# Expert rows scaled at their tile and scatter-added into one sum over a copy of x, output projections moved to the next even unit

## The reference

```python
xn = (x - mean) / sqrt(var + 1e-5)
# local attention: 16 heads of 16, windows of 128 tokens at a stride of 64
qkv = xn @ w_qkv + b_qkv
for each window:  ow = softmax(q k^T / 4) v
attn = (concat(windows) @ w_out + b_out)[:, :512]
# 8 experts of width 512, the best 2 of each row
p, i = softmax(top_k(xn @ gate_w.T, 2))
h1, h2 = split(xn @ w12[e].T)
y = sum over the row's two experts e of p_e * ((silu(h1) * h2) @ w3[e].T)
out = x + attn + y
```

## Time and profile before

| | |
|---|---|
| median of 3 runs | 704.5 us (704.3 to 704.83) |
| the profiled execution's own time | 704.97 us |
| its span | 703.2 us |
| busy: PE, PEld, DVE, ACT, POOL | 630.0, 509.7, 567.5, 513.2, 281.5 us |
| instructions: PE, DVE, ACT, POOL | 5914, 902, 882, 330 |
| memory read, written | 58.93, 32.83 MB |

### The profile page before, as it was taken

The page is one execution under the profiler, slowest core; times in us unless marked ns, Lnnn a source line. Parts: engine busy times, 40 slices in busy tenths (PEclk is TensorE's granted clock), DMA queues, the critical chain, the costliest instruction groups (busy, mean ns, idle before and its releaser), DMA issues.

```text
span 703.2 us, 17940 instructions
## 1 busy us (share of the span) xinstructions
PE 630.0 (90%) x5914; PEld 509.7 (72%) x5915; DVE 567.5 (81%) x902; ACT 513.2 (73%) x882; POOL 281.5 (40%) x330
## 2 busy tenths in 40 slices
PE   0786785989999999999999999999999999999985
PEld 0554564765888888888888888888767676666663
DVE  4968899986888888888888888888587979788884
ACT  4554578396787787777877877777577788888885
...
GB/s 299 263 257 193 110 251 305 121 314 48 53 52 52 60 52 52 59 48 57 53 52 60 52 53 60 52 52 54 38 192 242 180 246 209 262 228 159 207 141 31
DMA packets 66337, 92.62 MB, mean 132 GB/s; under 512 B 6432, under 2 KB 53408, under 8 KB 66272
## 3 DMA queue, kind: packets, MB, share of 16 engines
...
HBM read 58.93 MB, written 32.83 MB: 130 GB/s over the span
## 4 chain that ended last, share of the span: by engine, by line
PE 65%; DVE 14%; ACT 10%; issue 7%; POOL 2%; DMA 1%; ACTq 0%; DVEq 0%; POOLq 0%
PE PS L1319 57%; PE PS L1570 4%; DVE SMALL L980 4%; ACT WORK L785 3%; PE PS L1548 2%; DVE XN L1138 2%; DVE WALL L974 2%; ACT QS L780 1%; DMA XN<-in_x 1%; DVE WORK L1049 1%; DVE WORK L1042 1%; ACT WORK L723 1%; DVE WALL L998 1%; ACT SIDE L792 1%; POOL OTS L595 1%
## 5 line engine op out<-in xcount | busy, mean ns | idle before, releaser
L367 DVE TENSOR_TENSOR WS<-WALL,WS 128x1024 fp32r<-128x1024 f32 x134 | 164.4, 1227 | 55.2 <-ACT WS L877 40.8
L1319 PE MATMUL PS<-WS,XTS 128*128 128x512 f32 x804 | 203.9, 402 | 0.0
L1319 PEld LDWEIGHTS PS<-WS,XTS 128*128 128x128 f32 x804 | 146.2, 189 | 30.5
L877 ACT ACTIVATE WS<-WALL 128x1024 fp32r x134 | 141.6, 1056 | 8.8 <-issue 0.3
L1319 PE MATMUL PS<-DOWN_HIGH,HTS 128*128 x568 | 115.9, 289 | 0.8 <-ACT HTS L892 0.8
L595 POOL TENSOR_TENSOR OTS<-SIDE,XN 128x256 f32<-128x256 f32 x30 | 22.8, 761 | 205.2 <-DVE XN L1138 138.5
L1319 PEld LDWEIGHTS PS<-DOWN_HIGH,HTS 128*128 128x128 f32 x568 | 90.9, 188 | 1.6 <-issue 1.5
L980 DVE TENSOR_REDUCE SMALL<-PS 128x8 f32<-128x1024 f32 x64 | 77.5, 1211 | 12.2 <-PE PS L1319 11.9
L785 ACT ACTIVATE WORK<-PS 128x512 f32<-128x512 f32 x128 | 69.4, 595 | 23.6 <-PE PS L1319 20.3
L667 POOL DMA_INDIRECT ys_scratch<-SIDE,SIDX x36 | 43.8, 1218 | 93.2 <-ACT SIDE L908 93.2
L663 POOL DMA_INDIRECT XS<-xn_scratch,GIDX x71 | 71.8, 1011 | 23.0 <-issue 21.3
...
## 6 DMA issues: line engine op xcount, KB each, us to landing
...
WALL<-ys_scratch SPq DMA_DIRECT2D x16, 512.0 KB, 7.2
...
WALL<-in_x SPq DMA_DIRECT2D x8, 512.0 KB, 5.9
...
```

Of the source, the lines that this page charges most:

```text
L367: eng.tensor_tensor(out=WS[:, 1 - k, half, 1], in0=weights, in1=WS[:, 1 - k, half, 0].bitcast(F32), op=ALU.subtract).then_inc(low_ready[ha ...
L877: act.activation(WS[:, 1 - k, half, 0], weights, ACT.Copy).then_inc(high_ready[half], 1)
L1319: return pe.matmul(o, a, b, start=start, stop=stop)
```

## The change

**The sum lies in memory.** sum_scratch takes the place of ys_scratch and rows_scratch: 4096 rows and the dump rows. SP copies x into it (copy_x, eight copies of 512 KB from memory to memory). POOL adds the finished rows of batches 0 and 1 (keep, now a DMA that adds). Each scatter adds its tile's rows. Since a row's two experts may lie in any two tiles, scatter j waits for scatter j-1 to land, and scatter 0 for the copies and both keeps.

**Rows scaled at the tile.** xn_scratch has two more columns, the first share and the difference of the second to it. ACT stores them by a DMA in batch 0, unit 5 (4096 rows of two words). The gather brings them with the row, POOL picks the right one by KIND (find_share, one column), and ACT's copy out of PSUM (take_y) multiplies by it.

**Stage 1.** rest(b) is one load, of the sum. ACT's scale and POOL's combine are gone. POOL adds the bias (own), for batches 2 to 7. Batch 2's rest stands in the middle of begin(2). Batches 0 and 1 go from sum_scratch to the output by one copy each.

**Projections.** PE projects a window in the even unit behind its division's unit, behind that unit's queries_keys or values and ahead of its scores. DVE adds the result in that unit, behind the maxima and ahead of the next window's reciprocal.

The diff, cut:

```diff
@@ -41,7 +41,8 @@
-DUMP_ROW = 2 * B * L
+DUMP_ROW = B * L
+ROW = D + 2
@@ -56,9 +57,6 @@
-OWN = 3
-LATER = {4: 2, 5: 0, 6: 1}
-FIRST_LATER = min(LATER)
@@ -114,13 +112,10 @@
-        xn_dram = nc.dram_tensor("xn_scratch", (B * L, D), F32, kind="Internal").ap()
-        ys_dram = nc.dram_tensor("ys_scratch", (DUMP_ROW + SLOT_TILES * P, D), F32, kind="Internal").ap()
+        xn_dram = nc.dram_tensor("xn_scratch", (B * L, ROW), F32, kind="Internal").ap()
+        sum_dram = nc.dram_tensor("sum_scratch", (DUMP_ROW + SLOT_TILES * P, D), F32, kind="Internal").ap()
...
-        rows_dram = nc.dram_tensor("rows_scratch", (EXTRA * L, D), F32, kind="Internal").ap()
@@ -159,7 +154,9 @@
-        PW = sb("PW", [P, 2, NT])
+        PW = sb("PW", [P, NT, 2])
+        KIND = sb("KIND", [P, XS_TILES])
+        SHARE = sb("SHARE", [P, 2])
@@ -256,9 +253,7 @@
-        YG = WALL[:, 0:2 * NT * D].rearrange("p (t k d) -> p t k d", k=2, d=D)
-        XR = WALL[:, 2 * NT * D:].rearrange("p (t d) -> p t d", d=D)
+        XR = WALL[:, 0:NT * D].rearrange("p (t d) -> p t d", d=D)
...
-            yv = ys_dram[0:DUMP_ROW].rearrange("(k t p) d -> p t k d", k=2, p=P)
+            def copy_x(b):
+                r = slice(b * L, (b + 1) * L)
+                sp.dma_start(sum_dram[r], x[r]).then_inc(x_copied[b], 16)
             def rest(b):
                 t = slice(b * TB, (b + 1) * TB)
-                sp.dma_start(XR[:, t, :], xv[:, t, :]).then_inc(rest_in[b], 16)
-                for k in range(2):
-                    sp.dma_start(YG[:, t, k, :], yv[:, t, k, :]).then_inc(rest_in[b], 16)
-            def rows_back(b):
-                t = slice(b * TB, (b + 1) * TB)
-                sp.dma_start(XN[:, t, :], rv[:, t, :]).then_inc(rows_in[b], 16)
-                rest(b)
+                sp.dma_start(XR[:, t, :], sv[:, t, :]).then_inc(rest_in[b], 16)
@@ -469,16 +458,14 @@
+                    if b == EXTRA and half == 0:
+                        sp.wait_ge(y_stored, 1)
+                        rest(EXTRA)
...
-            def keep(b):
-                sp.wait_ge(r_free, (b + 1) * NWIN + 1)
-                t = slice(b * TB, (b + 1) * TB)
-                sp.dma_start(rv[:, t, :], XN[:, t, :]).then_inc(rows_out, 16)
@@ -488,34 +475,24 @@
-            keep(0)
-            load_tokens(2)
-            keep(1)
-            sp.wait_ge(rows_out, 16 * EXTRA)
-            sp.wait_ge(y_stored, 1)
+            load_tokens(EXTRA)
+            for b in range(B):
+                copy_x(b)
+            sp.wait_ge(phase_done, 3)
             sp.dma_start(KS[STK:DEEP, 1], KS[STK:DEEP, 0]).then_inc(hot_back, 16)
...
-            def send_later(n, b):
-                sp.wait_ge(later_ready, (n + 1) * TB)
-                t = slice(b * TB, (b + 1) * TB)
-                sp.dma_start(ov[:, t, :], XR[:, t, :]).then_inc(out_done, 16)
             for b in range(EXTRA, LAST):
                 begin(b)
                 rest(b + 1)
                 if b < LAST - 1:
                     load_tokens(b + 1)
-                if b + 2 in LATER:
-                    if LATER[b + 2] < EXTRA:
-                        rows_back(LATER[b + 2])
-                    else:
-                        rest(LATER[b + 2])
-                if b > OWN:
+                if b == EXTRA:
+                    for src in range(EXTRA):
+                        r = slice(src * L, (src + 1) * L)
+                        sp.dma_start(out[r], sum_dram[r]).then_inc(out_done, 16)
+                else:
                     send(b - 1)
-                    if b - 1 in LATER:
-                        send_later(b - 1 - FIRST_LATER, LATER[b - 1])
             send(LAST - 1)
-            send_later(LAST - 1 - FIRST_LATER, LATER[LAST - 1])
             for n in range(NWIN):
@@ -604,28 +581,18 @@
-            def combine(t, first, ready):
-                total = XR[:, t, :]
-                link(pool.tensor_tensor(out=total, in0=total, in1=first, op=ALU.add))
-                link(pool.tensor_tensor(out=total, in0=total, in1=YG[:, t, 0, :], op=ALU.add))
-                pool.tensor_tensor(out=total, in0=total, in1=YG[:, t, 1, :], op=ALU.add).then_inc(ready, 1)
+            def keep(b):
+                pool.wait_ge(r_free, (b + 1) * NWIN + 1)
+                pool.wait_ge(x_copied[b], 16)
+                t = slice(b * TB, (b + 1) * TB)
+                pool.dma_start(sum_dram[0:B * L].rearrange("(t p) d -> p t d", p=P)[:, t, :], XN[:, t, :],
+                               accum_op=ALU.add).then_inc(rows_out[b], 16)
             def own(b, n):
-                pool.wait_ge(own_scaled, 2 * ((b - OWN) * TB + n + 1))
-                pool.wait_ge(rest_in[b], 48)
-                combine(b * TB + n, BOUT[:], own_ready)
-            def later(b, n):
-                pool.wait_ge(later_scaled, 2 * ((b - FIRST_LATER) * TB + n + 1))
-                src = LATER[b]
-                pool.wait_ge(rest_in[src], 48)
-                if src < EXTRA:
-                    pool.wait_ge(rows_in[src], 16)
-                else:
-                    pool.wait_ge(r_free, src * NWIN + n + 2)
-                combine(src * TB + n, XN[:, src * TB + n, :], later_ready)
+                pool.wait_ge(rest_in[b], 16)
+                t = b * TB + n
+                pool.tensor_tensor(out=XR[:, t, :], in0=XR[:, t, :], in1=BOUT[:], op=ALU.add).then_inc(own_ready, 1)
@@ -664,33 +631,51 @@
             def scatter(j):
-                pool.indirect_dma_start(ys_dram, bass.IndirectOffsetOnAxis(SIDX[:, j:j + 1], 0),
-                                        YS[j % 2], None).then_inc(y_out[j % 2], 16)
+                if j:
+                    pool.wait_ge(y_out[1 - j % 2], 16 * ((j + 1) // 2))
+                else:
+                    for b in range(B):
+                        pool.wait_ge(x_copied[b], 16)
+                    for b in range(EXTRA):
+                        pool.wait_ge(rows_out[b], 16)
+                pool.indirect_dma_start(sum_dram, bass.IndirectOffsetOnAxis(SIDX[:, j:j + 1], 0),
+                                        YS[j % 2], None, compute_op=ALU.add).then_inc(y_out[j % 2], 16)
+            def find_share(j):
+                k = j % 2
+                pool.wait_ge(xs_in[k], 16 * (j // 2 + 1))
+                pool.tensor_scalar(out=SHARE[:, k:k + 1], in0=XS[:, k, D + 1:ROW], scalar1=KIND[:, j:j + 1],
+                                   scalar2=XS[:, k, D:D + 1], op0=ALU.mult, op1=ALU.add).then_inc(share_ready, 1)
+                pool.wait_ge(share_ready, j + 1)
             pool.wait_ge(map_done, 1)
             for blk in range(4):
                 pool.wait_ge(parts_out[blk], PARTS_OUT[blk // 2] * (EXTRA + 1))
+            pool.wait_ge(shares_out, 16)
             gather(0)
             gather(1)
             divide(6)
             divide_halves(7)
+            find_share(0)
+            find_share(1)
             pool.wait_ge(xt_full, 1)
             gather(2)
+            for b in range(EXTRA):
+                keep(b)
             for j in range(SLOT_TILES):
                 if j + 3 < SLOT_TILES:
                     pool.wait_ge(xt_full, j + 2)
                     gather(j + 3)
                 pool.wait_ge(ys_ready, j + 2)
                 scatter(j)
+                if j + 2 < SLOT_TILES:
+                    find_share(j + 2)
             for k in range(2):
                 pool.wait_ge(y_out[k], 16 * ((SLOT_TILES + 1 - k) // 2))
             pool.sem_inc(y_stored, 1)
             for b in range(EXTRA, B):
                 for n in range(NWIN):
-                    if b in LATER:
-                        later(b, n)
-                    if b >= OWN:
-                        own(b, n)
+                    own(b, n)
                     if b * NWIN + n < B * NWIN - 1:
@@ -820,14 +800,14 @@
-                    if b in LATER and u % 2 == 0:
-                        scale(LATER[b] * TB + u // 2, LATER[b], later_scaled)
-                    if b >= OWN and u % 2 == 1:
-                        scale(b * TB + u // 2, b, own_scaled)
+                    if b == 0 and u == 5:
+                        act.wait_ge(shares_made, 1)
+                        act.dma_start(xn_dram.rearrange("(t p) d -> p t d", p=P)[:, :, D:ROW], PW[:]
+                                      ).then_inc(shares_out, 16)
@@ -905,7 +885,8 @@
                     act.wait_ge(y_full, j + 1)
                     wait_some(act, y_out[k], 16 * stored)
-                    act.activation(YS[k], bank(7)[:, 0:D], ACT.Copy).then_inc(ys_ready, 1)
+                    act.wait_ge(share_ready, j + 1)
+                    act.activation(YS[k], bank(7)[:, 0:D], ACT.Copy, scale=SHARE[:, k:k + 1]).then_inc(ys_ready, 1)
...
                 link(dve.reciprocal(out=M2, in_=M1))
-                link(dve.tensor_copy(PW[:, 0, :], M2))
-                link(tt(PW[:, 1, :], E2, M2, ALU.mult))
+                link(dve.tensor_copy(PW[:, :, 0], M2))
+                link(tt(M1, E2, M2, ALU.mult))
+                link(tt(PW[:, :, 1], M1, M2, ALU.subtract))
```

(26 more changed lines are left out.)

24 lines of the change are left out of this document (10 added, 14 removed).

## The result

The changed kernel takes 721.1 us (median of 4 runs, 719.5 to 724.6). The kernel before took 704.4 us beside it. The ratio is 1.0244, with a 95% interval of 1.0206 to 1.0282: **slower by 16.7 us, 2.4%**. The profiled execution took 720.66 us, with a span of 718.9 us against 703.2, so its 15.7 us can be laid out in the trace.

A forecast was written before the change was run, and what follows sets the result against it. PE bounds the expert loop, a chain through ACT, DVE and POOL the last stage; 1.4 + 0.2 + 4 + 0 + 2.6 + 2.6 - 0.8 = +10.0 on 704.97 gives 715.0 us, range 705 to 728.

The forecast's parts named there:

- 1. Shares: Stage 0: ACT's new DMA of the shares costs 1.4 us, DVE's small extra operation 0.2 us.
- 2. Copies and kept rows: Start of the loop: transfers ending beyond 171 us delay PE once, 4 us lost, bounds 0 and 12.
- 3. Inside the loop: Expert loop: POOL's idleness covers the share, an adding scatter lands in about 3.8 us, so 0 us.
- 4. Entry to batch 2: POOL's bias addition waits for a load and delays the first division; PE loses 2.6 us.
- 5. The batches: Last stage: DVE's addition ahead of the reciprocal makes batches 34.4 us each, four batches 2.6 us slower.
- 6. The last batch: Last batch: ACT's chain loses its scalings, 0.8 us gained, bounds 0 and 2.6.
- Serial scatters: Expert loop: adding scatters take over 4.84 us and set the pace; 53 us, about 765 in all; chance 0.12.
- Light batches: Batches 3 to 7: DVE reaches the reciprocal no later, all batches at 33.07 us, 700.4 in all; chance 0.10.

The follow-up runs named there:

- e1: Changed kernel with the projections back at the end of the odd units, on PE and DVE: 716.4 us.
- e2: Kernel before with only the projections moved to the even units: 713.4 us, ratio 1.0130.
- e10: Changed kernel with DVE's addition of the projection behind the reciprocal in place of ahead of it, PE unchanged: 723.9 us.
- e3: Changed kernel with the eight copies of x moved earlier, four at about 56 us and four at about 126 us: 714.7 us.
- e8: e7 with gather 3 back in the loop, kept rows stored plainly by SP, their sum's rows added to the output in batches 3 and 4: 710.6 us.
- e7: Changed kernel with odd-unit projections, batch 2's additions behind its divisions, gather 3 ahead of kept rows, all copies of x at about 126 us: 717.0 us.
- e4: Changed kernel with POOL's bias additions of batch 2 behind the divisions of the same windows: 719.8 us.
- e9: e8 with the copies of x at about 56 and 126 us and POOL's eight pieces in the last batch: 702.6 us, ratio 0.9975.
- e5: Changed kernel with the gather of tile 3 ahead of the two adding transfers of kept rows: 725.5 us.

## Why the prediction was right, and where it was off

The direction and the range (705 to 728) held: 721.1 us. The sum said +10.0, and the trace has +15.7. The sum held no term for PE's clock, which fell behind two of PE's waits and cost 3.9 us at the start of the loop and 2.0 at the entry to batch 2. That is about as much as the whole difference of 5.7, but the other terms were off as well, both ways. By its steps:

**1. Shares: near in size by luck, wrong in place.** It charged 1.4 us to ACT's DMA and 0.2 to DVE's operation. The loop starts 2.1 us later, but the DMA took 0.39 us of the queue. What is visible is the slot map's wait for the moved addition, 2.0 us longer (2.62 - 0.59), which the prediction missed: it followed the move of the projection through stage 1 alone. e1 (0.69), e2 (2.69) and e10 (4.68) show that this wait follows the addition. What the shares cost by themselves was not tried alone. e1, which has them and not the wait, starts the loop 0.5 us later than the kernel before, which is inside the scatter of that start.

**2. Copies and kept rows: this term was mis-sized, 4 for 9.2 us.** The prediction asked when the ten transfers end, with 168.3 us as the low end, from 395 GB/s; its 4 us stand for 175. The second kept rows landed near 179.5 (173.45 + 6.0). It missed three things. Gather 2 runs among the copies and lands 6 us late, so PE loses 2.10 us before any kept row matters. And POOL's queue takes a second transfer of 512 KB only once the first has landed, so the adds follow each other and not the copies' bandwidth. And of the 9.16 us only 5.3 are waits, the thing that the term priced; 3.9 are the same matmuls at a lower clock. That gather 3 and scatter 0 stand behind the adds was foreseen. e3 gives 7.3 of the 9.2 to the copies, and e8 the rest to the adds.

The price of an add can be read where little else moved. The second kept rows of the kernel before, stored plainly at 156.27, and those of the changed kernel, added at 173.45:

```profile
rows_scratch<-XN SPq DMA_DIRECT2D x1, 512.0 KB, 3.5
```
```profile
sum_scratch<-XN POOLq DMA_DIRECT2D x1, 512.0 KB, 6.0
```

In e8 the plain store at 161.04 took 3.4 us, and in e3 and e7 the second add took 5.9 and 6.0. (The first plain store of each kernel ran among the weight loads and took 10.1 and 10.8.) So an add of 512 KB takes 2.5 us more, 1.7 times as long. A scatter of 128 KB went from 2.8 to 3.9 us.
The Trainium skill (Collectives: The Full Stack, The bandwidth ceiling) says of the adding step of a collective that it sends two read descriptors for each chunk and has half the rate of a copy. The trace is near that: 6.0 against 3.5 us from issue to landing. The two also differ in their queue, POOL's and SP's, and no run separates the queue from the add.

**3. Inside the loop: right.** Tiles are 4.84 us apart (319.40 us for 66, from tile 4 to tile 70), an add lands in 3.9 us (forecast about 3.8), and that stretch is as long as before to 0.1 us. The cover was thinner than said: the share takes 1.7 us and not 0.5, a scatter's issue 1.6 and not 1.3, and 0.7 us of POOL's idleness is left.

**4. Entry to batch 2: the wait was right, the clock was left out.** The first division comes 2.7 us behind its reciprocal. The entry costs 3.5 (forecast 2.6), but only 1.5 of that is idle PE and 2.0 is the lower clock behind the wait, so the nearness of the total is partly luck. e4 gets 2.3 back. The stretch from the last tile to the first reciprocal adds 0.63, which the prediction put at 0.

**5. The batches: right in mechanism, twice too large.** The term said 2.6, from 1.3 per batch for the addition and 0.9 back. Its excess of 1.4 hides part of what step 2 lacks. Measured: 1.0 for the addition (e1, e2 and e10 agree to 0.1 in the first three distances; the last has 0.7, 1.1 and 0.8), and 0.95 back from the load taken off POOL and ACT in batches 4 to 6, so only the first distance pays, 1.0, and in all 1.2. Of the three additions ahead of a reciprocal, each of 0.45, a little over two come through.

**6. The last batch: right.** -0.78 for -0.8, and the copies into SIDE are 6.45, 6.43 and 6.23 us apart, where the prediction said some 6.3.

**The rivals.** Serial scatters: no, 3.9 us is below 4.84. (Its price was a little off as well: 53 us and the sum's 10 make 768, not 765.) Light batches: its price was exact and its condition was not met. With the projections in the odd units (e1) all pitches are 33.05 to 33.06 but the last, against the rival's 33.07. So the sum in memory does make the batches lighter, and the moved addition takes that away. In e9 the rival's case exists, and it is worth 0.25% rather than the 0.6% that the rival gave, since the start of the loop and the entry still cost something.

**What stays open.** Why the loop starts up to 3.5 us apart in kernels that are alike up to there. The clock is part of it: 0.97 or 0.83 and 0.74 from 110 to 120 us, and in e5 the slot map's 36 matmuls took 3.37 us at 0.69, against 2.42 in the changed kernel. But the length of the wait ahead doesn't decide it: e3 waited 3.07 us for the same addition, as e5 did with 3.08, and its 36 matmuls took 2.42. What makes the executions part, before 85 us, was not found. How the cost of an add splits between the add and POOL's queue is open as well.
